# A GRU behind a mixture of experts: the order of VectorE's waits, and idle matmuls in every chunk

## The chip, the cores and the metric

The kernel runs on one core of a Trainium2 chip. The metric is the time of one execution on the device in microseconds (us); the time of the kernel before is the median of 3 runs.

## The reference

The input x has 2 sequences of 1024 tokens with 256 features. A first layer adds to each token the output of a mixture of experts (four experts and a shared branch, each 256 to 1024 to 256 with gelu). The experts' weights come from one gate per sequence, the two best of four, and two experts are masked over a third of the tokens each:

```
for e in range(E):
    h = gelu(x @ ew1[e] + eb1[e]);  y = h @ ew2[e] + eb2[e]
    out = out + w_be[:, e] * mask[e] * y
x = x + out + (gelu(x @ sw1 + sb1) @ sw2 + sb2)
```

A second layer is a recurrence over the 1024 tokens, whose state h has 256 features for each of the two sequences, and its output is added to x:

```
z = sigmoid(x_t @ W_z + h @ U_z + vz)
r = sigmoid(x_t @ W_r + h @ U_r + vr)
hh = tanh(x_t @ W + (r * h) @ U + vh)
h = (1 - z) * h + z * hh
```

Step t + 1 needs h of step t, and within a step hh needs r.

## The kernel before

**Stages.** The 1024 tokens are cut into 16 chunks of 64 (CT = 64, CH = 16). After a setup (x transposed, the gate computed, the first chunk's experts, weights of the recurrence split in two 16-bit parts) the recurrence runs from step s = 0 to 1023, with c = s // 64 the chunk and t = s % 64 the step in it. The weights of all experts stay on the chip.

**One step.** TensorE multiplies h by U_r (12 small matmuls at L781: for two output and two input halves the high part of h by two weight parts, and then the low part, h_low, by one), then by U_z (12 more), and later p = (1 + tanh_r) * h by U (12 more, into c_ps). The results are added in PSUM to the projections of x. ScalarE takes the tanh of each sum (L402). VectorE computes p_cur (L594) and its low part p_low (L597) after tanh r, the two parts of blend (L602, L604) after tanh z, and after tanh c the new state by one scan (L610, h_cur), then h_low (L613), half_h (L614) and the output row (L619).

**Side work.** Between the matmuls of z and those of c (window 0) and between those of c and the next step's r (window 1) TensorE has slots for the next chunk's work: one unit in window 0, two in window 1. The units, in a list SIDE written out ahead, are the halves of the up- and down-projections of 40 hidden tiles (UP at L688, DOWN at L706, 128x128 f32), their bias (L717) and the projections of x onto the gates (PROJECT, L722). Steps 0 to 55 hold the experts' units, steps 57 to 60 the projections. Every 16 steps (t = 1, 17, 33, 49) window 1 also holds a TURN, the transposes of 16 finished output rows (L728). No unit stands in window 1 of step 55, in both windows of step 56 and in both windows of steps 61, 62 and 63. ScalarE runs a gelu (L396) for each finished up-projection after the tanh of c, and GpSimd scales the hidden tile by the expert's weight (L275).

**The last chunk** has no next chunk. There each window ends in idle matmuls at L813 (a 128x128 bf16 identity by constants, into a bank whose content nobody needs): one of 256 columns in window 0, two of 512 in window 1. Other chunks have none.

**Order and waits.** Each engine runs its own list in order. preact counts the finished gate sums, act_done the tanhs, part_ready the parts of p and h, blended the blends and half_h. VectorE's p_cur, blend and scan each wait for two of these, written one after the other: first for VectorE's own earlier result (part_ready or blended), then for ScalarE's tanh (act_done, at L593, L601 and L609). TensorE's first weight load of c waits for p_cur, that of r for the scan.

Of the kernel before, what the change touches and what calls it, by code (L numbers as in the profile page):

```python
# [16 lines left out]
GATES = 3  # L17
R, Z, C = range(GATES)
# [6 lines left out]
STEPS = 16  # L25
# [11 lines left out]
def moe_gru_kernel(nc, x, cond, gate_w, gate_b, time_w, time_b, ew1, eb1, ew2, eb2, sw1, sb1, sw2, sb2,  # L37
                   w_z, u_z, c_z, b_z, w_r, u_r, c_r, b_r, w_h, u_h, c_h, b_h, branch_mask, out):
    B, T, D = x.shape
    E, _, H = ew1.shape  # L40
    BR = E + 1
    KC = D // P
    CT = TOKENS
    CH = T // CT
# [38 lines left out]

    UP, DOWN, BIAS, TURN, PROJECT = "up", "down", "bias", "turn", "project"
    SIDE = {(t, w): [] for t in range(CT) for w in range(2)}
    for t in range(1, CT, STEPS):
        SIDE[t, 1].append((TURN, 0, 0))
    units = []
    for i in range(BR * HT + LAG):
        if i < BR * HT:  # L90
# [32 lines left out]
    with ctx:  # L123
# [6 lines left out]
        def sem(name):  # L130
            return ctx.enter_context(nc.semaphore(name))
# [122 lines left out]
        act_done = sem("act_done")  # L254
# [172 lines left out]
        def _(dve):  # L427
# [151 lines left out]
            def side(c, t, window):  # L579
                if c == CH - 1:  # L580
                    return
                if (t, window) in SEEDS:
                    seed(c + 1, *SEEDS[t, window])
                if t == RESIDUAL_STEP:
                    residual(c + 1, window)

            sq = lambda ap: ap.rearrange("p (m b) -> p m b", b=B)
            for s in range(T):
                c, t = divmod(s, CT)
                parts = s * PARTS_STEP  # L590

                dve.wait_ge(part_ready, parts + H_HIGH)
                dve.wait_ge(act_done, s * GATES + R + 1)  # L593
                dve.scalar_tensor_tensor(p_cur[:, :, 0:B], sq(tanh_r), 1.0, sq(h_now), ALU.add, ALU.mult  # L594
                                         ).then_inc(part_ready, 1)
                dve.wait_ge(part_ready, parts + PARTS_STEP + P_HIGH)
                dve.tensor_tensor(p_low[:, :, 0:B], p_cur[:, :, 0:B], p_bits[:, :, 1:2 * B:2], ALU.subtract  # L597
                                  ).then_inc(part_ready, 1)

                dve.wait_ge(blended, (s + 1) * BLEND_STEP)  # L600
                dve.wait_ge(act_done, s * GATES + Z + 1)  # L601
                dve.scalar_tensor_tensor(blend_v[:, :, 0], tanh_z, 1.0, half_s[:, :], ALU.add, ALU.mult  # L602
                                         ).then_inc(blended, 1)
                dve.scalar_tensor_tensor(blend_v[:, :, 1], tanh_z, 1.0, half_h[:, :], ALU.subtract, ALU.mult  # L604
                                         ).then_inc(blended, 1)
                side(c, t, 1)

                dve.wait_ge(blended, (s + 1) * BLEND_STEP + 2)
                dve.wait_ge(act_done, s * GATES + C + 1)  # L609
                dve.tensor_tensor_scan(h_cur[:, 0, :], cand, blend[:, :], 0.0, ALU.mult, ALU.add  # L610
                                       ).then_inc(part_ready, 1)
                dve.wait_ge(part_ready, parts + PARTS_STEP + H_HIGH)
                dve.tensor_tensor(h_low[:, 0, :], h_now, h_high, ALU.subtract).then_inc(part_ready, 1)  # L613
                dve.tensor_scalar(half_h[:, :], h_now, -0.5, None, ALU.mult).then_inc(blended, 1)  # L614

                body, row = divmod(s, STEPS)
                if row == 0 and body >= 2:
                    dve.wait_ge(turned, body - 1)
                last = dve.scalar_tensor_tensor(  # L619
                    out_feat[:, body % 2, :, row * B:(row + 1) * B], sq(h_now), h_unscale[:, :],  # L620
                    feat[:, :, s * B:(s + 1) * B], ALU.mult, ALU.add)
                if row == STEPS - 1:
                    last.then_inc(body_added, 1)

                if t < CT - 1:
                    side(c, t + 1, 0)

        @block.tensor
        def _(pe):
# [50 lines left out]
            def up(c, i, k):  # L680
                e, j = TILES[c][i]
                n = TILE0[c] + i
                if k == 0:
                    if c <= 1 and j == 0:
                        pe.wait_ge(up_in[e], 16)
                    if n >= 2:
                        pe.wait_ge(gelu_done, n - 1)
                last = mm(up_ps[n % 2][:, 0:COLS], up_w[:, e, k, j * P:(j + 1) * P],  # L688
                          feat[:, k, c * COLS:(c + 1) * COLS], start=(k == 0), stop=(k == KC - 1),
                          skip_group_check=True)  # L690
                if k == KC - 1:
                    last.then_inc(up_done, 1)

            def down(c, i, m):
                e, j = TILES[c][i]
                n = TILE0[c] + i
                if m == 0:
                    if c <= 1 and j == 0:
                        pe.wait_ge(down_in[e], 16)
                    if e == E:  # L700
                        pe.wait_ge(gelu_done, n + 1)
                    elif c == 0:
                        pe.wait_ge(scaled_first, SCALED[n])
                    else:
                        pe.wait_ge(scaled, SCALED[n])
                last = mm(y_ps[:, m * COLS:(m + 1) * COLS], down_w[:, e, j, m * P:(m + 1) * P],  # L706
                          hidden[:, n % TILES_HELD, :], start=False, stop=(m == KC - 1), skip_group_check=True)
                if m == KC - 1:
                    last.then_inc(down_done, 1)

            def output_bias(c, m):
                if m == 0:
                    if c > 0:
                        pe.wait_ge(feat_ready, c * KC)
                    if c <= 1:
                        pe.wait_ge(rows_made, c + 1)
                mm(y_ps[:, m * COLS:(m + 1) * COLS], bias2_rows[:, m * P:(m + 1) * P],  # L717
                   branch_rows[:, c * COLS:(c + 1) * COLS], start=(m == 0), stop=False, skip_group_check=True)

            def project(c, g, m, k):  # L720
                at = (c % 2) * REGION + m * COLS
                mm(gate_ps[g][:, at:at + COLS], wx[:, g, k, m * P:(m + 1) * P], feat[:, k, c * COLS:(c + 1) * COLS],  # L722
                   start=False, stop=False, skip_group_check=True)

            def turn_body(n):
                pe.wait_ge(body_added, n + 1)
                for k in range(KC):
                    last = pe.transpose(rows_ps[:, k * P:(k + 1) * P], out_feat[:, n % 2, k, :], ident[:, :])  # L728
                last.then_inc(turned, 1)
# [54 lines left out]
            def side(c, t, window):  # L784
                for what, *of in SIDE[t, window]:
                    if what == TURN:
                        n = c * BODIES + t // STEPS
                        if n > 0:

                            pe.wait_ge(blended, (c * CT + t + 1) * BLEND_STEP + 2)  # L790
                            if n > 1:
                                pe.wait_ge(turned_copied, n - 1)
                            turn_body(n - 1)
                    elif c < CH - 1:
                        i, k = of[0], of[1]
                        if what == UP:
                            up(c + 1, i, k)
                        elif what == DOWN:
                            down(c + 1, i, k)
                        elif what == BIAS:  # L800
                            output_bias(c + 1, k)
                        else:
                            g, m, k = of
                            if m == 0 and k == 0:
                                pe.wait_ge(feat_ready, (c + 2) * KC)
                                pe.wait_ge(seeded, (c + 2) * GATES * KC)
                            if g == Z and k == 0:

                                pe.wait_ge(act_done, (c * CT + t) * GATES + Z + 1)
                            project(c + 1, g, m, k)  # L810
                if c == CH - 1:
                    for _ in range(1 + window):
                        mm(up_ps[0][:, 0:IDLE_FILL[window]], ident16[:, :], keep_warm[:, 0:IDLE_FILL[window]],  # L813
                           start=True, stop=True, skip_group_check=True)

            for s in range(T):
                c, t = divmod(s, CT)
# [52 lines left out]
```

## Time and profile before

| | us |
|---|---|
| median of 3 runs | 2193.73 (2191.86 to 2194.32) |
| the profiled execution's own time | 2188.36 |
| its span in the profile | 2186.6 |
| first scan (L610) starts at | 68.43 |
| last scan starts at | 2182.25 |
| TensorE busy with matmuls | 2097.8 (96%) |
| VectorE busy | 1225.8 (56%) |
| ScalarE busy | 690.5 (32%) |
| GpSimd busy | 216.9 (10%) |

Times inside the profile count from the start of its span. PE is TensorE's matmuls, PEld its weight loads, DVE is VectorE, ACT ScalarE, POOL GpSimd. Durations of matmuls are modelled, so the starts are the better guide there. The granted clock (PEclk) is that of TensorE, as a share of full speed (2.4 GHz); 0.50 is 1.2 GHz. A view of stretches gives for each stretch its length, then for each engine the busy time with the number of instructions in brackets, then the granted clock, the share of the DMA engines and GB/s. Since each step has one scan, the scans in a stretch count its steps. DMA plays no part after the setup: 3 to 5 GB/s.

### The profile page before, as it was taken

The page shows a single profiled execution, that of the slowest core. Times are in us where ns is not written, and L with a number is a line of the kernel's source. Part 1 is how long each engine was busy: PE and PEld are TensorE (multiplying, and loading weights), DVE is VectorE, ACT ScalarE, POOL GpSimd, SP SyncE. Part 2 cuts the span into 40 slices and gives each one's busy share as a digit, 9 for nine tenths or more (in the row PEclk, how much of TensorE's full clock was granted, in tenths as well). Part 3 has the DMA queues.
Part 4 walks back from the last instruction along what each step waited for, and adds up shares of the span by engine and source line. Part 5 has one row for each costly group of instructions (what it writes and reads, how often), then busy time and mean ns, then how long its engine had stood idle before and what let it go on. Part 6 is the DMA issues. An engine that isn't in the chain of part 4 may idle for free.

```text
span 2186.6 us, 102353 instructions
## 1 busy us (share of the span) xinstructions
PE 2097.8 (96%) x42772; PEld 1805.8 (83%) x42772; DVE 1225.8 (56%) x8413; ACT 690.5 (32%) x3780; POOL 216.9 (10%) x520
## 2 busy tenths in 40 slices
PE   8899999999999999999999999999999999999998
PEld 8788888888888888888888888888888888888655
DVE  4465655556565564655656555565555656556554
ACT  3232323323233232333323233232332323333222
POOL 2210101001010010101101011010100101011000
PEclk9998988979799797998989989798897989979899
DMA  7000000000000000000000000000000000000000
GB/s 276 3 4 4 5 3 4 5 3 5 3 5 4 3 4 4 4 4 4 4 4 5 4 4 4 4 5 3 4 5 3 4 4 4 4 4 4 4 4 4
DMA packets 16908, 23.66 MB, mean 11 GB/s; under 512 B 3584, under 2 KB 15159, under 8 KB 16444
## 3 DMA queue, kind: packets, MB, share of 16 engines
q1 hardware_dynamic: 15280, 17.05, 2.2%
q8 instruction: 334, 5.47, 1.0%
q14 instruction: 130, 1.06, 0.2%
q10 hardware_dynamic: 1164, 0.07, 0.0%
HBM read 15.01 MB, written 2.10 MB: 8 GB/s over the span
## 4 chain that ended last, share of the span: by engine, by line
PE 91%; DVE 3%; ACT 2%; issue 2%; POOL 1%; DVEq 0%; ACTq 0%
PE r_ps L781 20%; PE c_ps L781 18%; PE up_ps L688 17%; PE y_ps L706 16%; PE z_ps L781 13%; ACT rc_tanh_ps L402 2%; PE c_ps L722 1%; PE r_ps L722 1%; DVE h_cur L610 1%; PE z_ps L722 1%; DVE p_cur L594 1%; PE y_ps L717 1%; PE z_tanh_ps L728 1%; POOL uf L340 0%; ACT hidden L396 0%
## 5 line engine op out<-in xcount | busy, mean ns | idle before, releaser
L688 PE MATMUL up_ps<-feat,up_w 128*128 128x128 f32 x2528 | 550.9, 319 | 2.3 <-ACT hidden L396 1.0
L706 PE MATMUL y_ps<-hidden,down_w 128*128 128x128 f32 x2528 | 528.3, 307 | 0.0
L610 DVE TENSOR_TENSOR_SCAN h_cur<-rc_tanh_ps,blend 128x8 f32<-128x8 f32 x1024 | 177.6, 173 | 484.8 <-ACT rc_tanh_ps L402 483.5
L781 PEld LDWEIGHTS r_ps<-h_cur,u_high 128*128 128x128 f16 x4096 | 260.4, 98 | 223.5 <-DVE h_cur L610 223.3
L781 PE MATMUL r_ps<-h_cur,u_high 128*128 128x20 bf16 (+5 forms) x4096 | 355.3, 181 | 47.8 <-DVE h_cur L610 42.4
L688 PEld LDWEIGHTS up_ps<-feat,up_w 128*128 128x128 f32 x2528 | 389.5, 205 | 9.6 <-ACT hidden L396 8.9
L402 ACT ACTIVATE rc_tanh_ps<-r_ps 128x4 f32<-128x4 f32 x1024 | 161.8, 158 | 729.2 <-PE r_ps L781 729.1
L781 PE MATMUL c_ps<-p_cur,u_high 128*128 128x40 bf16 (+10 forms) x4096 | 363.6, 186 | 20.1 <-DVE p_cur L594 14.5
L706 PEld LDWEIGHTS y_ps<-hidden,down_w 128*128 128x128 f32 x2528 | 369.0, 194 | 3.3 <-issue 2.2
L594 DVE SCALAR_TENSOR_TENSOR p_cur<-rc_tanh_ps,h_cur 128x4 f32<-128x4 f32 x1024 | 166.9, 163 | 364.3 <-ACT rc_tanh_ps L402 359.5
L781 PEld LDWEIGHTS c_ps<-p_cur,u_high 128*128 128x128 f16 x4096 | 263.6, 98 | 107.6 <-DVE p_cur L594 39.0
L781 PE MATMUL c_ps<-p_cur,u_mid 128*128 128x40 bf16 (+10 forms) x4096 | 346.3, 182 | 0.0
L402 ACT ACTIVATE rc_tanh_ps<-c_ps 128x4 f32<-128x4 f32 x1024 | 161.8, 158 | 583.0 <-PE c_ps L781 583.0
L781 PE MATMUL r_ps<-h_cur,u_mid 128*128 128x20 bf16 (+5 forms) x4096 | 338.3, 178 | 0.0
L781 PE MATMUL z_ps<-h_cur,u_high 128*128 128x20 bf16 (+5 forms) x4096 | 337.5, 178 | 0.0
L781 PE MATMUL z_ps<-h_cur,u_mid 128*128 128x20 bf16 (+5 forms) x4096 | 336.9, 178 | 0.0
L275 POOL TENSOR_TENSOR hidden<-hidden,expert_w 128x128 f32<-128x128 f32 (+3 forms) x416 | 163.1, 394 | 1572.2 <-ACT hidden L396 1572.2
L781 PEld LDWEIGHTS c_ps<-p_cur,u_mid 128*128 128x128 f16 x4096 | 269.6, 99 | 5.8
L781 PEld LDWEIGHTS r_ps<-h_cur,u_mid 128*128 128x128 f16 x4096 | 263.0, 98 | 6.3 <-issue 0.3
L614 DVE TENSOR_SCALAR half_h<-h_cur 128x4 f32<-128x4 f32 x1024 | 267.4, 261 | 0.5
L781 PE MATMUL c_ps<-p_low,u_high 128*128 128x40 f16 (+10 forms) x4096 | 264.5, 181 | 0.2
L781 PEld LDWEIGHTS z_ps<-h_cur,u_high 128*128 128x128 f16 x4096 | 254.3, 97 | 0.0
(138 smaller groups left out, 3063.4 us busy)
## 6 DMA issues: line engine op xcount, KB each, us to landing
up_w<-in_L_cond_ew SPq DMA_DIRECT2D x4, 1024.0 KB, 9.3
down_w<-in_L_cond_ew SPq DMA_DIRECT2D x4, 1024.0 KB, 11.0
x_rows<-in_x SPq DMA_DIRECT2D x8, 256.0 KB, 4.4
out<-out_rows SPq DMA_DIRECT2D x128, 16.0 KB, 1.8
up_w<-in_L_cond_sw SPq DMA_DIRECT2D x1, 1024.0 KB, 12.1
down_w<-in_L_cond_sw SPq DMA_DIRECT2D x1, 1024.0 KB, 13.6
cf<-in_L_cond_C_r SPq DMA_DIRECT2D x1, 256.0 KB, 5.8
cf<-in_L_cond_C_z SPq DMA_DIRECT2D x1, 256.0 KB, 5.9
```

The source lines that it names most:

```text
L275: ins = engine.tensor_tensor(cols, cols, w, ALU.mult)
L402: act.activation((tanh_r, tanh_z, c_now)[g].rearrange("p (m b) -> p m b", b=B), gate_v[g][:, c % 2, :, t, :], ACT.Tanh, scale=0.5 / GAIN). ...
L594: dve.scalar_tensor_tensor(p_cur[:, :, 0:B], sq(tanh_r), 1.0, sq(h_now), ALU.add, ALU.mult).then_inc(part_ready, 1)
L610: dve.tensor_tensor_scan(h_cur[:, 0, :], cand, blend[:, :], 0.0, ALU.mult, ALU.add).then_inc(part_ready, 1)
L614: dve.tensor_scalar(half_h[:, :], h_now, -0.5, None, ALU.mult).then_inc(blended, 1)
L688: last = mm(up_ps[n % 2][:, 0:COLS], up_w[:, e, k, j * P:(j + 1) * P], feat[:, k, c * COLS:(c + 1) * COLS], start=(k == 0), stop=(k == KC ...
L706: last = mm(y_ps[:, m * COLS:(m + 1) * COLS], down_w[:, e, j, m * P:(m + 1) * P], hidden[:, n % TILES_HELD, :], start=False, stop=(m == KC ...
L717: mm(y_ps[:, m * COLS:(m + 1) * COLS], bias2_rows[:, m * P:(m + 1) * P], branch_rows[:, c * COLS:(c + 1) * COLS], start=(m == 0), stop=Fal ...
L722: mm(gate_ps[g][:, at:at + COLS], wx[:, g, k, m * P:(m + 1) * P], feat[:, k, c * COLS:(c + 1) * COLS], start=False, stop=False, skip_group ...
L728: last = pe.transpose(rows_ps[:, k * P:(k + 1) * P], out_feat[:, n % 2, k, :], ident[:, :])
L781: return mm(gate_ps[g][:, at:at + width], w[:, g, k, m * P:(m + 1) * P], moving, start=False, stop=last_of_sum, skip_group_check=True)
```

## The change

On VectorE the two waits ahead of p_cur, ahead of the first blend and ahead of the scan change places: the one for ScalarE's tanh (act_done) is now written first, the one for VectorE's own result second. On TensorE a slot with nothing in it but perhaps a TURN (real == 0) gets idle matmuls in every chunk, where before only the last chunk had them: one of 256 columns in window 0, two of 512 columns in window 1, and one fewer in a window that has a turn. The latter holds in the last chunk too, whose four windows with a turn so lose one of their two idle matmuls. TURNS lists the slots with a turn.

```diff
-    for t in range(1, CT, STEPS):
-        SIDE[t, 1].append((TURN, 0, 0))
+    TURNS = [(t, 1) for t in range(1, CT, STEPS)]
+    for slot in TURNS:
+        SIDE[slot].append((TURN, 0, 0))
...
+                dve.wait_ge(act_done, s * GATES + R + 1)
                 dve.wait_ge(part_ready, parts + H_HIGH)
-                dve.wait_ge(act_done, s * GATES + R + 1)
                 dve.scalar_tensor_tensor(p_cur[:, :, 0:B], sq(tanh_r), 1.0, sq(h_now), ALU.add, ALU.mult
                                          ).then_inc(part_ready, 1)
...
+                dve.wait_ge(act_done, s * GATES + Z + 1)
                 dve.wait_ge(blended, (s + 1) * BLEND_STEP)
-                dve.wait_ge(act_done, s * GATES + Z + 1)
                 dve.scalar_tensor_tensor(blend_v[:, :, 0], tanh_z, 1.0, half_s[:, :], ALU.add, ALU.mult
                                          ).then_inc(blended, 1)
...
+                dve.wait_ge(act_done, s * GATES + C + 1)
                 dve.wait_ge(blended, (s + 1) * BLEND_STEP + 2)
-                dve.wait_ge(act_done, s * GATES + C + 1)
                 dve.tensor_tensor_scan(h_cur[:, 0, :], cand, blend[:, :], 0.0, ALU.mult, ALU.add
                                        ).then_inc(part_ready, 1)
...
-                if c == CH - 1:
-                    for _ in range(1 + window):
+
+                real = 0 if c == CH - 1 else sum(what != TURN for what, *_ in SIDE[t, window])
+                turning = (t, window) in TURNS
+                if real == 0 or c == CH - 1:
+                    for _ in range(1 + window - turning):
                         mm(up_ps[0][:, 0:IDLE_FILL[window]], ident16[:, :], keep_warm[:, 0:IDLE_FILL[window]],
                            start=True, stop=True, skip_group_check=True)
```

## Rows read from the trace of the kernel before

**Rows 1.** The page: TensorE's busy tenths and granted clock in 40 slices.

```profile
PE   8899999999999999999999999999999999999998
PEclk9998988979799797998989989798897989979899
```

**Rows 2.** Stretches: opening, openings and ends of chunks, middles, last chunk.

```profile
68.43:76.90 8.47, 7.94 (x169) 6.90 (x167) 4.79 (x32) 2.99 (x16) 1.56 (x4) 1.00 0.01 2
329.18:343.52 14.34, 14.24 (x212) 12.67 (x212) 6.20 (x40) 3.82 (x21) 1.56 (x4) 0.50 0.01 3
346.03:443.37 97.34, 96.63 (x2057) 83.42 (x2055) 58.20 (x398) 33.74 (x185) 10.81 (x27) 1.00 0.02 4
443.37:462.77 19.40, 16.23 (x352) 14.46 (x353) 9.83 (x74) 4.27 (x27) 0.00 (x0) 0.75 0.01 2
1144.13:1241.35 97.22, 96.19 (x2054) 83.14 (x2052) 58.17 (x400) 33.57 (x184) 10.41 (x26) 1.00 0.02 4
1807.32:1903.94 96.62, 96.06 (x2060) 83.30 (x2056) 58.44 (x399) 33.56 (x185) 10.40 (x26) 1.00 0.02 4
2063.12:2182.25 119.13, 107.92 (x2347) 67.33 (x2346) 62.40 (x480) 29.35 (x183) 0.00 (x0) 1.00 0.02 4
```

**Rows 3.** Waits: engine, line, releaser: total us, times, longest us.

```profile
DVE h_cur L610 <- ACT rc_tanh_ps L402: 483.5, 1010, 1.0
DVE p_cur L594 <- ACT rc_tanh_ps L402: 359.5, 987, 12.2
PEld r_ps L781 <- DVE h_cur L610: 223.3, 911, 0.9
PEld up_ps L688 <- ACT hidden L396: 8.9, 16, 0.6
```

**Rows 4.** Timeline of one step at full clock: start, us, engine, instruction.

```profile
1100.77 0.16 ACT L402 ACTIVATE rc_tanh_ps<-c_ps 128x4 f32<-128x4 f32 x1 [0.52 <-PE c_ps L781]
...
1101.03 0.17 DVE L610 TENSOR_TENSOR_SCAN h_cur<-rc_tanh_ps,blend 128x8 f32<-128x8 f32 x1 [0.45 <-ACT rc_tanh_ps L402]
...
1101.76 0.16 ACT L402 ACTIVATE rc_tanh_ps<-r_ps 128x4 f32<-128x4 f32 x1 [0.55 <-PE r_ps L781]
...
1101.88 0.47 PE L688 MATMUL up_ps<-feat,up_w 128*128 128x128 f32 x2
1102.02 0.16 DVE L594 SCALAR_TENSOR_TENSOR p_cur<-rc_tanh_ps,h_cur 128x4 f32<-128x4 f32 x1 [0.41 <-ACT rc_tanh_ps L402]
...
1102.24 0.19 PE L781 MATMUL c_ps<-p_cur,u_high 128*128 128x40 bf16 x1
1102.28 0.18 PE L781 MATMUL c_ps<-p_cur,u_mid 128*128 128x40 bf16 x1
```

**Rows 5.** Line L593: instruction, count, ns min/median/max, first and last start.

```profile
L593 DVEq EVENT_SEMAPHORE  x1024: 21/21/21, 67.4 to 2181.2; - x171
```

**Rows 6.** Timeline in the setup: a feat copy and the reduction behind it.

```profile
12.00 0.63 ACT L379 ACTIVATE feat<-z_tanh_ps 128x512 f32<-128x512 f32 x1 [0.21 <-PE z_tanh_ps L641]
12.66 0.86 DVE L461 TENSOR_REDUCE seg_part<-feat 128x4 f32<-128x680 f32 x1 [0.76 <-ACT feat L379]
```

**Rows 7.** Timeline of TensorE in chunk 1, step 4: side pair, then r.

```profile
204.89 0.49 PE L706 MATMUL y_ps<-hidden,down_w 128*128 128x128 f32 x2
205.22 0.18 PE L781 MATMUL r_ps<-h_cur,u_high 128*128 128x20 bf16 x1
205.25 0.18 PE L781 MATMUL r_ps<-h_cur,u_mid 128*128 128x20 bf16 x1
```

**Rows 8.** Timeline of scans at half clock: without idle matmuls, and with them.

```profile
458.29 0.17 DVE L610 TENSOR_TENSOR_SCAN h_cur<-rc_tanh_ps,blend 128x8 f32<-128x8 f32 x1 [0.55 <-ACT rc_tanh_ps L402]
460.41 0.17 DVE L610 TENSOR_TENSOR_SCAN h_cur<-rc_tanh_ps,blend 128x8 f32<-128x8 f32 x1 [0.55 <-ACT rc_tanh_ps L402]
...
2058.46 0.17 DVE L610 TENSOR_TENSOR_SCAN h_cur<-rc_tanh_ps,blend 128x8 f32<-128x8 f32 x1 [0.55 <-ACT rc_tanh_ps L402]
...
2061.15 0.17 DVE L610 TENSOR_TENSOR_SCAN h_cur<-rc_tanh_ps,blend 128x8 f32<-128x8 f32 x1 [0.22 <-ACT rc_tanh_ps L402]
```

## The prediction

> **What bounds the kernel now.** I read the page first. TensorE is busy 96% of the span, which seems to say that only less matmul work can help, but the line of its granted clock beside it is not even: it stands at 9 to 10 tenths with a dip to 7 about every two and a half slices, and a chunk of 64 steps lasts about as long [rows 1]. So I cut the span by stage and counted the scans (L610, one for each step) in each stretch [rows 2]. With side work and the full clock (1.00 of full speed, 2.4 GHz) 49 steps take 97.34, 97.22 and 96.62 us in three chunks, 1.981 us a step. In the last nine steps of a chunk, six of which have slots without side work, the mean clock is 0.75 and nine steps take 19.40 us (2.16 each). In the next opening the clock is 0.50 (1.2 GHz) and five steps take 14.34 us (2.87 each), though TensorE has all its side work again. The last chunk has no side work anywhere and idle matmuls in its place: 60 steps in 119.13 us, 1.986 each, the clock at 1.00 throughout.
>
> The step therefore does not depend on how much TensorE has to do at full clock: 1.98 us both with side work (TensorE busy 96.63 of 97.34 us) and with the lighter idle matmuls (107.92 of 119.13 us) [rows 2]. A fixed length under different loads is a chain of latencies. The list of waits names it: VectorE waits for ScalarE's tanh 483.5 us ahead of the scan and 359.5 us ahead of p_cur, and TensorE's weight load then waits for h_cur 223.3 us [rows 3]. The timeline of one step gives its links [rows 4]: tanh of c starts at 1100.77 and ends at 1100.93, the scan starts at 1101.03; tanh of r runs from 1101.76 to 1101.92, p_cur starts at 1102.02, and c's first matmul at 1102.24. Both hand-overs from ScalarE to VectorE take 0.10 us.
>
> **The waits on VectorE.** The line of the second of each pair of waits (L593, the tanh's semaphore) is an instruction of its own on VectorE's queue, 1024 times, 21 ns each [rows 5]; so the wait written first rides on the arithmetic instruction, and the one written second is this separate instruction in front of it. In the kernel now the late event (tanh) is the separate one: VectorE must see it pass and only then start p_cur, 0.10 us after the tanh's end. The change swaps the roles at three places (L594, L602, L610). A wait for ScalarE that rides on the instruction is in the trace too: in the setup a feat copy ends at 12.00 + 0.63 = 12.63 and the reduction that waits for it starts at 12.66, 0.03 us later [rows 6]. So a hand-over should fall from 0.10 to 0.03 us, by 0.07. The bounds: nothing, if the riding wait behaves otherwise in this dense loop, and 0.08 by the rounding of these rows; I take 0.07, because the row is the same pair of engines. The part_ready and blended waits that now come as instructions of their own are for VectorE's own results, done half a microsecond before the tanh, and their 21 ns pass while VectorE is idle; if they were late, each would cost its 21 ns. Queued behind each are p_low, h_low and the rest of the step; they only come earlier. The third place (L602, blend) is not on the chain: its result is needed by the scan half a microsecond later. It counts as nothing.
>
> What is late next? After the scan, TensorE: its weight load waited 223.3 us for h_cur in 911 steps, 0.245 us each [rows 3], so 0.07 fits whole. Ahead of c there is less. The pair of side matmuls starts at 1101.88 and c's first and second matmuls come at 1102.24 and 1102.28, 0.36 and 0.40 later [rows 4]. Where TensorE is the bound, the same pair starts at 204.89 and the next matmuls at 205.22 and 205.25, 0.33 and 0.36 later [rows 7]; there the pair follows another f32 pair and lasts 0.49, here it follows a bf16 matmul and lasts 0.47, so here 0.34 would do. p_cur can come 0.04 to 0.06 us earlier before the side work is the bound, with perhaps all 0.07 where the weight load is hidden. I take 0.065. Per step 0.07 + 0.065 = 0.135 us, bounds 0 and 0.14 us.
>
> In sentences the rest can do without: the Trainium skill, "Advanced Engine Details and Errata", gives 50 to 100 ns for a sequencer that reads a semaphore's value. By it two such reads a step, 1024 times, would be an estimated 102 to 205 us against the 138 us of the rows; the rows lie inside.
>
> **The idle matmuls.** Slots without side work are the second slot of step 55, both of 56 and both of 61, 62 and 63: nine in each of 15 chunks, 4 with one 256-column matmul and 5 with two of 512 columns, so 14 matmuls and as many weight loads a chunk, 210 in all; the last chunk loses four (one in each slot with a turn). At full clock they cost nothing, since the last chunk keeps 1.986 us a step with just these in every slot [rows 2]; that cover is the same latency chain, with p_cur now 0.07 earlier, and a 256-column fill ends before f32 side work does. What they should bring is the clock: the last chunk holds 1.00 for 119 us on recurrence and fill alone, and side steps hold it for 97 us [rows 2], so no slot would be left in which TensorE does less than something that was seen to hold it. Then the opening also runs at full clock. How that looks chunk 0 shows, which opened at 1.00: its steps 1 to 4 take 8.47 us [rows 2], so steps 2 to 4 take 8.47 - 1.97 = 6.50. This is no clock: the up-projections stand close there, and TensorE waits for ScalarE's gelu once a chunk, 8.9 us in 16 waits [rows 3], and for longer bias units. Of these three steps I take off only one hand-over each: 6.50 - 0.21 = 6.29. The four dropped matmuls in the last chunk gain under 0.1 us.
>
> **The sum**, against the profiled execution (span 2186.6, its own time 2188.36 us):
> - to the first scan 68.43 - 0.14 = 68.3;
> - 1023 further steps, of which 15 x 3 = 45 are the crowded ones of the openings: 978 x (1.981 - 0.135) = 978 x 1.846 = 1805.4;
> - 15 x 6.29 = 94.4;
> - after the last scan 2186.6 - 2182.25 = 4.35, unchanged.
>
> That is a span of 1972.4, and with the 1.8 us outside it 1974.2. The runs' median of 2193.73 lies 5.4 above the profiled execution; with a steadier clock I expect a smaller distance and take 2: **1976 us**. Of the 214 us gained some 135 come from the waits and some 77 from the clock.
>
> **Rivals.**
> 1. The clock still falls at every chunk's end, so the idle matmuls do nothing. For it: it falls now although TensorE is busy 16.23 of 19.40 us there [rows 2]. Against it: the last chunk. Steps at half clock are bound by TensorE and gain little from the waits. Of 1024 steps some 850 are at full clock (all but about eleven a chunk) and gain 0.135 us each, 115 us: 2188.4 - 115 = 2073, less a little for the others: about 2071. The Trainium skill, "TensorE: Matmul & The Clock Gate" (section "Why this matters for your kernels"), puts drops of the clock down to idle gaps between bursts of matmuls. By that rule alone it would not fall here at all, since the weight load's waits in these steps are fractions of a microsecond, and fillers would have nothing to mend; the trace disagrees, so I give the rule little weight.
> 2. It holds at the chunk's end but dips in the openings: five steps at half clock in 14.34 us [rows 2] instead of the 9.9 that the sum has (6.29 and two of 1.846), 15 x 4.4 = 66 us: 2042 if in all, about 2000 if in a third of them.
> 3. The waits bring nothing, because VectorE's start after the tanh takes 0.10 us whichever wait rides on it (the change doesn't do what it says): 68.4 + 978 x 1.981 + 15 x 6.5 + 4.4 + 1.8 = 2109.5.
> 4. Slower: the clock does not hold, and each fill then runs at half clock. In the last chunk's beginning, at half clock, a step with fill takes 2061.15 - 2058.46 = 2.69 us, while one without any takes 460.41 - 458.29 = 2.12 [rows 8]. 0.57 us in five steps (56, 61 to 63 and the one after 55) of 15 chunks is 43 us: about 2232. It decides the sign only if a hand-over gains less than 43 / 2048 = 21 ns.
>
> **How the numbers follow.** The forecast (full clock, both waits) has 0.75 with an own range of 1950 to 1995; rival 2 has 0.10, rival 1 0.08, rival 3 0.05, rival 4 0.02. The range of 1948 to 2045 takes in the forecast and rival 2 and leaves about 0.15 outside; its low end is a step of 1.82 us (both hand-overs 0.07 to 0.08 and fewer stalls). About 0.2% is what a measurement of this kernel can tell from no change. All cases but the fourth are far below: faster 0.97, same 0.01, slower 0.02.
>
> **What would show it.** In the profile after: the separate wait instruction at the part_ready line instead of the tanh's, and 0.03 us from a tanh's end to p_cur and to the scan; 1.84 to 1.85 us a step in the middle of a chunk; the line of the granted clock at 9 or full without the regular 7s; about 400 idle matmuls (192 + 206); the list's wait of TensorE for h_cur nearly as large and for p_cur still small. I am wrong if the step stays near 1.98 (the waits), if c's first matmul follows the side pair with no gap and the step stands above 1.86 (TensorE as the bound), or if stretches at 0.50 remain in the chunks' ends or openings.

## The result and the profile after

| | us |
|---|---|
| kernel before, beside these runs | 2193.10 (4 runs, 2191.86 to 2194.32) |
| changed kernel | 1969.23 (4 runs, 1968.59 to 1972.54) |
| ratio | 0.8982, 95% interval 0.8967 to 0.8998 |
| profiled execution of the changed kernel, its span | 1969.39, 1967.6 |

The change takes off 10.2%; 1976 us was forecast, with a range of 1948 to 2045. Most lines of the code have moved down by one: the separate wait L593 is now L594, p_cur L595, the scan L611, the small matmuls L782, the idle matmuls L817.

The page, TensorE's busy tenths and granted clock in 40 slices. The regular 7s of [rows 1] are gone:

```profile
PE   8899999999999999999999999999999999999998
PEclk9999999999999999999999999999999999999999
```

Stretches as in [rows 2] (length, then busy time and count of PE, PEld, DVE, ACT, POOL, granted clock, DMA share, GB/s): chunk 0's steps 1 to 4; then, each of seven steps, an opening at part of the clock (chunk 2) and one at the full clock (chunk 5); then 48 steps of chunk 5's middle, the nine behind them (from the scan of step 55 to that of the next chunk's step 0, called the last nine below), and 58 steps of the last chunk.

```profile
66.37:74.48 8.11, 7.58 (x168) 6.89 (x168) 4.48 (x32) 2.99 (x16) 1.60 (x4) 1.00 0.01 2
302.68:317.39 14.71, 14.48 (x296) 13.28 (x296) 8.11 (x56) 5.22 (x28) 2.35 (x6) 0.88 0.02 5
660.23:673.85 13.62, 13.39 (x296) 12.14 (x296) 8.10 (x56) 5.22 (x28) 2.35 (x6) 1.00 0.02 5
673.85:761.90 88.05, 87.98 (x2016) 81.72 (x2016) 55.44 (x390) 33.06 (x181) 10.42 (x26) 1.00 0.02 5
761.90:778.30 16.40, 16.13 (x364) 12.88 (x366) 9.75 (x75) 4.27 (x27) 0.00 (x0) 1.00 0.01 2
1850.67:1957.08 106.41, 101.77 (x2237) 64.59 (x2265) 60.36 (x464) 28.78 (x178) 0.00 (x0) 1.00 0.02 5
```

A step of the middle is 88.05 / 48 = 1.834 us instead of 1.981, and one of the last chunk 106.41 / 58 = 1.835. The nine steps at a chunk's end take 16.40 us (1.82 each) at a clock of 1.00, where they took 19.40 at 0.75. The opening takes 13.62 us where its first five steps alone took 14.34. In 8 of the 15 chunks that have side work the clock still falls once in the opening, in step 4 and for 3.4 us, as in the second stretch, and costs 14.71 - 13.62 = 1.1 us. Such a short fall is called a dip below.

The last chunk's last three steps stand in a line of their own. The clock falls there in step 61, although that chunk has its idle matmuls in every slot:

```profile
1957.08:1963.08 6.00, 5.52 (x115) 3.82 (x117) 3.16 (x25) 1.42 (x9) 0.00 (x0) 0.63 0.01 4
```

It costs 0.6 us (steps 55 to 63 of that chunk take 17.0 us here and 16.4 in the repeated run below, where the clock holds). A fall in steps 59 to 62 of the last chunk is also in the profiles of e2, e3, e4, e5 and e10 below and in none of the others, so the idle matmuls hold the clock nearly always, not always. Their weight loads (L817) count 398, as forecast.

The line of the separate wait and the list of waits. The separate wait has moved from the tanh's line (L593 in [rows 5]) to the line of part_ready, and VectorE waits less than in [rows 3]:

```profile
L594 DVEq EVENT_SEMAPHORE  x1024: 21/21/21, 53.4 to 1961.2; - x171
```

```profile
DVE h_cur L611 <- ACT rc_tanh_ps L403: 379.9, 1008, 0.8
DVE p_cur L595 <- ACT rc_tanh_ps L403: 289.7, 975, 11.6
PEld r_ps L782 <- DVE h_cur L611: 71.9, 152, 0.6
```

TensorE's wait for h_cur, 223.3 us in 911 waits before, seems to be gone from nearly all steps. It is not: the list leaves out idle times of 0.15 us and less, and this one has fallen from 0.18 us to 0.11 in the middle of a chunk. The first weight load of r still comes 0.05 us after the scan's end, before (1101.03 + 0.17 = 1101.20) and after (995.58 + 0.17 = 995.75):

```profile
1101.26 0.10 PEld L781 LDWEIGHTS r_ps<-h_cur,u_high 128*128 128x128 f16 x1 [0.17 <-DVE h_cur L610]
...
995.80 0.10 PEld L782 LDWEIGHTS r_ps<-h_cur,u_high 128*128 128x128 f16 x1
```

The timeline of one step, the counterpart of [rows 4]. The tanh of r ends at 994.47 + 0.16 = 994.63 and p_cur starts at 994.66; the tanh of c ends at 995.54 and the scan starts at 995.58: 0.03 and 0.04 instead of 0.10 and 0.10. The side pair starts at 994.59 and c's first two matmuls at 994.89 and 994.92, 0.30 and 0.33 later instead of 0.36 and 0.40:

```profile
994.47 0.16 ACT L403 ACTIVATE rc_tanh_ps<-r_ps 128x4 f32<-128x4 f32 x1 [0.76 <-PE r_ps L782]
...
994.59 0.47 PE L707 MATMUL y_ps<-hidden,down_w 128*128 128x128 f32 x2
994.66 0.16 DVE L595 SCALAR_TENSOR_TENSOR p_cur<-rc_tanh_ps,h_cur 128x4 f32<-128x4 f32 x1 [0.34 <-ACT rc_tanh_ps L403]
...
994.89 0.18 PE L782 MATMUL c_ps<-p_cur,u_high 128*128 128x40 bf16 x1
...
994.92 0.18 PE L782 MATMUL c_ps<-p_cur,u_mid 128*128 128x40 bf16 x1
...
995.38 0.16 ACT L403 ACTIVATE rc_tanh_ps<-c_ps 128x4 f32<-128x4 f32 x1 [0.45 <-PE c_ps L782]
...
995.58 0.17 DVE L611 TENSOR_TENSOR_SCAN h_cur<-rc_tanh_ps,blend 128x8 f32<-128x8 f32 x1 [0.38 <-ACT rc_tanh_ps L403]
```

### The profile page after: what moved, and what is told of

Its sections match the earlier page's. It is cut to its first block, busy times and chain, and to the rows that moved or that the text cites. A ratio compares the mean times of both kernels' runs of the same rounds, so it can differ in the third digit from the quotient of the medians.

```text
span 1967.6 us, 102687 instructions
## 1 busy us (share of the span) xinstructions
PE 1936.1 (98%) x42900; PEld 1730.1 (88%) x42978; DVE 1188.4 (60%) x8413; ACT 689.9 (35%) x3780; POOL 216.6 (11%) x520
## 4 chain that ended last, share of the span: by engine, by line
PE 96%; issue 1%; POOL 1%; DVE 1%; ACT 1%; ACTq 0%; DVEq 0%
PE r_ps L782 20%; PE up_ps L689 18%; PE y_ps L707 18%; PE c_ps L782 16%; PE z_ps L782 16%; PE up_ps L817 4%; PE c_ps L723 1%; PE r_ps L723 1%; PE z_ps L723 1%; PE z_tanh_ps L729 1%; PE y_ps L718 1%; POOL uf L339 0%; POOL uf L341 0%; ACT hidden L397 0%; POOL wx L349 0%
## 5 line engine op out<-in xcount | busy, mean ns | idle before, releaser
L689 PE MATMUL up_ps<-feat,up_w 128*128 128x128 f32 x2528 | 519.2, 304 | 3.8 <-ACT hidden L397 3.8
L707 PE MATMUL y_ps<-hidden,down_w 128*128 128x128 f32 x2528 | 520.2, 303 | 0.0
L611 DVE TENSOR_TENSOR_SCAN h_cur<-rc_tanh_ps,blend 128x8 f32<-128x8 f32 x1024 | 177.3, 173 | 381.4 <-ACT rc_tanh_ps L403 379.9
L782 PEld LDWEIGHTS r_ps<-h_cur,u_high 128*128 128x128 f16 x4096 | 249.6, 96 | 162.6 <-DVE h_cur L611 71.9
L689 PEld LDWEIGHTS up_ps<-feat,up_w 128*128 128x128 f32 x2528 | 365.3, 193 | 8.7 <-ACT hidden L397 8.2
L782 PE MATMUL r_ps<-h_cur,u_high 128*128 128x20 bf16 (+5 forms) x4096 | 350.4, 180 | 3.1 <-DVE h_cur L611 0.7
L782 PE MATMUL c_ps<-p_cur,u_high 128*128 128x40 bf16 (+10 forms) x4096 | 343.3, 181 | 2.8
L595 DVE SCALAR_TENSOR_TENSOR p_cur<-rc_tanh_ps,h_cur 128x4 f32<-128x4 f32 x1024 | 166.0, 162 | 292.5 <-ACT rc_tanh_ps L403 289.7
L782 PE MATMUL c_ps<-p_cur,u_mid 128*128 128x40 bf16 (+10 forms) x4096 | 338.0, 180 | 0.0
L782 PE MATMUL r_ps<-h_cur,u_mid 128*128 128x20 bf16 (+5 forms) x4096 | 336.6, 178 | 0.0
L782 PE MATMUL z_ps<-h_cur,u_high 128*128 128x20 bf16 (+5 forms) x4096 | 336.0, 178 | 0.0
L782 PE MATMUL z_ps<-h_cur,u_mid 128*128 128x20 bf16 (+5 forms) x4096 | 335.4, 178 | 0.0
L620 DVE SCALAR_TENSOR_TENSOR out_feat<-h_cur,h_unscale,feat 128x4 f32<-128x4 f32 x1024 | 295.5, 289 | 0.0
L782 PEld LDWEIGHTS c_ps<-p_cur,u_high 128*128 128x128 f16 x4096 | 248.4, 96 | 40.6 <-DVE p_cur L595 26.7
L782 PE MATMUL c_ps<-p_low,u_high 128*128 128x40 f16 (+10 forms) x4096 | 259.5, 179 | 0.0
L782 PEld LDWEIGHTS r_ps<-h_cur,u_mid 128*128 128x128 f16 x4096 | 256.7, 96 | 1.1
L782 PEld LDWEIGHTS c_ps<-p_cur,u_mid 128*128 128x128 f16 x4096 | 256.5, 96 | 0.5
L782 PEld LDWEIGHTS z_ps<-h_cur,u_high 128*128 128x128 f16 x4096 | 251.8, 96 | 0.0
```

Of the source, the lines that this page charges most:

```text
L620: last = dve.scalar_tensor_tensor(out_feat[:, body % 2, :, row * B:(row + 1) * B], sq(h_now), h_unscale[:, :], feat[:, :, s * B:(s + 1) * ...
L782: return mm(gate_ps[g][:, at:at + width], w[:, g, k, m * P:(m + 1) * P], moving, start=False, stop=last_of_sum, skip_group_check=True)
```

## The experiments

**The two parts, each alone.** The kernel before with only the waits changed:

```diff
-                dve.wait_ge(part_ready, parts + H_HIGH)
                 dve.wait_ge(act_done, s * GATES + R + 1)
+                dve.wait_ge(part_ready, parts + H_HIGH)
...
(likewise ahead of the blend and of the scan; no idle matmuls added)
```

> The kernel before with only the order of the three waits changed. My theory: waits and clock are separate gains. The middle of a chunk falls from 1.981 to 1.834 us a step as in the changed kernel, the ends and openings of the chunks still run at half clock and gain little there: 2188 less 850 steps x 0.147 us, about 2060 us (2045 to 2075), mean granted clock 0.90 to 0.92. Rival: the shorter step packs TensorE densely enough to hold the clock without idle matmuls; then the clock is above 0.97 and the time below 1990 us.

And the changed kernel with the waits as before, so that only the idle matmuls remain:

```diff
-                dve.wait_ge(act_done, s * GATES + R + 1)
                 dve.wait_ge(part_ready, parts + H_HIGH)
+                dve.wait_ge(act_done, s * GATES + R + 1)
...
(likewise ahead of the blend and of the scan)
```

> The changed kernel with the order of the waits as before, so only the idle matmuls remain of the change. My theory: the clock holds except for short dips in openings (0.98), the step stays at 1.97 to 1.98 us: 2095 to 2112 us. Rival (the idle matmuls hold the clock only together with the shorter step): clock under 0.95 and 2150 us or more.

Measured beside the kernel before at 2191.62 us: 2053.34 us for the waits alone (ratio 0.9335, 0.928 to 0.939; the four runs go from 2030.51 to 2055.56) and 2115.52 us for the idle matmuls alone (0.9656, 0.9642 to 0.9671). Stretches of the waits-only kernel: the 48 middle steps of chunk 5, its last nine, and the seven of the next opening.

```profile
704.98:793.02 88.04, 87.81 (x2015) 81.67 (x2014) 55.41 (x391) 33.08 (x181) 10.45 (x26) 1.00 0.02 5
793.02:812.63 19.61, 17.02 (x352) 15.80 (x353) 9.88 (x74) 4.27 (x27) 0.00 (x0) 0.60 0.01 3
812.63:831.05 18.42, 18.32 (x297) 16.55 (x297) 8.19 (x56) 5.22 (x28) 2.35 (x6) 0.59 0.01 4
```

The middle is that of the changed kernel (88.04 us), the end and the opening are still at 0.60 and 0.59. The shorter step does not hold the clock. The idle-matmul kernel has the middle of the kernel before (first line of the next block) and a mean clock of 0.987; its time lies 3.5 us above the 2112 that I expected at most. So the waits are worth 138 us without and 146 us with the idle matmuls, and these 76 and 84 us: two gains that hardly touch.

**One hand-over at a time.** As the idle-matmul kernel, with only the waits ahead of p_cur, or only those ahead of the scan, changed:

```diff
+                dve.wait_ge(act_done, s * GATES + R + 1)
                 dve.wait_ge(part_ready, parts + H_HIGH)
-                dve.wait_ge(act_done, s * GATES + R + 1)
```

> As e2_fill_only, with the waits changed ahead of p_cur alone. My theory: 0.07 us a step off e2_fill_only, 70 to 75 us; TensorE's side work ahead of c ends just in time. Rival (side work in window 0 is the bound): 0.04 us a step or less, 40 us or less.

```diff
+                dve.wait_ge(act_done, s * GATES + C + 1)
                 dve.wait_ge(blended, (s + 1) * BLEND_STEP + 2)
-                dve.wait_ge(act_done, s * GATES + C + 1)
```

> As e2_fill_only, with the waits changed ahead of the scan alone. My theory: 0.07 us a step, 70 to 75 us off e2_fill_only, and the gains of e3 and e4 add up to the changed kernel within 5 us. Rival: one of the two gains is only had together with the other, so that they add up to 20 us less or more than the changed kernel has.

2037.18 us (0.9295, 0.9281 to 0.9308) and 2037.62 us (0.9298, 0.9284 to 0.9312): 78.3 and 77.9 us off 2115.52. The 48 middle steps of chunk 5, a stretch from each of the three kernels: idle matmuls alone,

```profile
722.13:817.42 95.29, 94.88 (x2017) 81.77 (x2015) 56.94 (x390) 33.09 (x181) 10.38 (x26) 1.00 0.02 4
```

with p_cur's waits,

```profile
696.98:788.57 91.59, 91.46 (x2017) 81.76 (x2015) 59.65 (x390) 33.09 (x181) 10.38 (x26) 1.00 0.02 4
```

with the scan's waits:

```profile
694.30:786.09 91.79, 91.54 (x2017) 81.72 (x2016) 55.50 (x391) 33.10 (x181) 10.41 (x26) 1.00 0.02 4
```

1.985, 1.908 and 1.912 us a step. Each hand-over gives 0.07 and a little more, and each kernel gains 3 us more than the 75 that I expected at most; side work in window 0 is no bound for p_cur. The two gains sum to 156.2 us where the changed kernel has 2115.52 - 1969.23 = 146.3, 10 us less, so the 5 us that I had allowed were too few. In the middles they do add up (95.29 - 91.59, 95.29 - 91.79 and 95.29 - 88.05: 3.70 + 3.50 = 7.20 against 7.24). The profiled executions differ in the dips of the clock instead: 8 with the idle matmuls alone (seven in openings and one in step 62 of chunk 13), 2 and 2 in these two kernels, 8 in the changed one. Summed as the gains are, that is 8 + 8 - 2 - 2 = 12 dips at some 0.9 to 1.1 us each. The openings bear it out: steps 0 to 7 of the 15 chunks take 250.2 us with the idle matmuls alone, 239.2 and 239.8 in these two kernels and 238.6 in the changed one, and 250.2 + 238.6 - 239.2 - 239.8 = 9.8.

**The third place.** The changed kernel with the waits ahead of the first blend in the old order:

```diff
-                dve.wait_ge(act_done, s * GATES + Z + 1)
                 dve.wait_ge(blended, (s + 1) * BLEND_STEP)
+                dve.wait_ge(act_done, s * GATES + Z + 1)
```

> The changed kernel with the waits ahead of the first blend (L602) in the old order. My theory: off the chain, no difference, 1966 to 1973 us. Rival: the late separate wait holds VectorE's queue ahead of the scan, and each step loses up to 0.07 us: 2000 to 2040 us.

1976.93 us (four runs, 1968.0 to 1978.61; ratio 0.9013, 0.899 to 0.9035), so the rival's 2000 is excluded, but the median is 8 us above the changed kernel, above my 1973. The profiled execution was the one of 1968.0 us: it has 3 dips of the clock where the changed kernel had 8, and a middle step that is 0.004 us longer. Two things make it so: stalls ahead of the scan that sum to 3.3 us instead of 0.9 (last section), and eight steps in which h_low, which TensorE needs for r, takes 0.39 to 0.41 us instead of 0.16. The line of h_low in this run, then in the changed kernel (duration in ns, min/median/max):

```profile
L614 DVE TENSOR_TENSOR h_low<-h_cur x1024: 161/164/405, 66.9 to 1961.8; 128x4 f16<-128x4 f32 x171
...
L614 DVE TENSOR_TENSOR h_low<-h_cur x1024: 161/165/165, 66.6 to 1963.3; 128x4 f16<-128x4 f32 x171
```

The other three executions ran at mean granted clocks of 0.984 to 0.986, where this one had 0.992. At 0.985 one execution of the changed kernel took 1972.54 us and one of these 1977.84. So some 5 us belong to the order at an equal clock, which fits 0.004 us in each of 1023 steps, and the rest of the 8 us to a lower clock, whose cause is open. The hand-over is not on the chain with its 0.07 us, but it does not count as quite nothing either.

**How much fill.** Idle matmuls of 64 and 128 columns in all chunks but the last:

```diff
+                        n_fill = IDLE_FILL[window] // (1 if c == CH - 1 else 4)
-                        mm(up_ps[0][:, 0:IDLE_FILL[window]], ident16[:, :], keep_warm[:, 0:IDLE_FILL[window]],
+                        mm(up_ps[0][:, 0:n_fill], ident16[:, :], keep_warm[:, 0:n_fill],
                            start=True, stop=True, skip_group_check=True)
```

> The changed kernel with idle matmuls of 64 and 128 columns in place of 256 and 512 in all chunks but the last. My theory: what counts is how much TensorE works, so the clock falls again in many chunk ends: granted clock 0.91 to 0.96, 2000 to 2060 us. Rival (closing the idle gap with any instruction is enough, as the rule on idle gaps would have it): as the changed kernel, 1969 us, clock 0.98 or more.

2031.44 us (0.9284, 0.9255 to 0.9313), mean clock 0.932. The last nine steps of chunk 5 and the seven of the next opening:

```profile
786.31:804.32 18.01, 16.23 (x364) 14.51 (x365) 9.81 (x75) 4.27 (x27) 0.00 (x0) 0.79 0.01 3
804.32:818.78 14.46, 14.26 (x297) 12.92 (x297) 8.11 (x56) 5.23 (x28) 2.36 (x6) 0.91 0.03 6
```

The number of instructions is that of the changed kernel, which has x364 in the same nine steps at a clock of 1.00; their length is a quarter, and the clock falls. It is not enough that something is issued in the gap.

**Where fill is needed.** Idle matmuls only in steps 61 to 63:

```diff
-                if real == 0 or c == CH - 1:
+                if (real == 0 and t > 60) or c == CH - 1:
```

> The changed kernel with idle matmuls only in steps 61 to 63 of the chunks before the last, none after step 55's first slot and in step 56. My theory: those two steps are enough for a fall of their own, as before in step 57; it is short, for the projections of steps 57 to 60 follow, and the fill then carries the clock into the next chunk: 2 to 3 us a chunk, 1995 to 2015 us, openings mostly at full clock. Rival: a fall at step 57 costs the opening too, 2030 us or more; or steps 55 and 56 are too short to matter, 1969 us.

1999.01 us (0.9134, 0.9117 to 0.9151), within the expectation. The one and a half empty steps 55 and 56 are enough to lose the clock around step 57, in 12 of the 15 chunks. Two ends of chunks, chunk 5's and chunk 7's:

```profile
776.71:794.22 17.51, 16.60 (x362) 13.95 (x363) 9.76 (x74) 4.27 (x27) 0.00 (x0) 0.90 0.01 3
1015.15:1035.46 20.31, 19.48 (x361) 16.41 (x362) 9.88 (x75) 4.27 (x27) 0.00 (x0) 0.60 0.01 2
```

With the same work and the same fill one end has 0.90 and the other 0.60: how long a fall lasts depends on more than the work in it.

**The crowded openings.** The bias units moved from before tile 3's down-projection to behind tile 1's up-projection:

```diff
-        if i == LAG:
+        if i == 1:
             units += [(BIAS, 0, 0), (BIAS, 0, 1)]
```

> The changed kernel with the two bias units placed after the up-projections of tile 1, so that those of tile 2 come after the gelu of tile 0 is done. My theory: TensorE's wait for the gelu makes step 2 long (2.22 us) and is also what the clock dips in step 4 or 5 follow. Without it step 2 falls by about 0.3 us and no chunk opens with a dip: 15 x 0.3 plus 8 dips x 1.06 us, about 1955 to 1961 us, clock 0.99. Rival: the dips follow the crowded bias steps instead; they remain, and the gain is at most 5 us, 1964 us or more.

And with both bias units in window 1:

```diff
-        if i < BR * HT:
+        if i == 1:
+            units += [(UP, 1, 0), (BIAS, 0, 1), (UP, 1, 1)]
+        elif i < BR * HT:
             units += [(UP, i, 0), (UP, i, 1)]
-        if i == LAG:
-            units += [(BIAS, 0, 0), (BIAS, 0, 1)]
+        if i == 0:
+            units += [(BIAS, 0, 0)]
```

> As e7, but both bias units in window 1, where TensorE has 0.08 us of slack ahead of r. If a bias unit costs less there than ahead of c, it is 2 to 4 us faster than e7 (1952 to 1958 us); if the crowding of a turn or an up-projection with a bias unit ahead of r costs as much, it is the same as e7 within 2 us.

1956.39 us (0.8929, 0.8913 to 0.8945) and 1955.06 us (0.8922, 0.8907 to 0.8938). The first is as long as expected, but not by the steps I named: its opening of chunk 5 takes 13.22 us, 0.40 less than 13.62, while step 2 stays at 2.21 us and steps 3 and 4 fall from 2.03 to 1.84 and 1.83. Both bias units now stand between the scans of steps 1 and 2. TensorE's wait for the gelu is gone (8.2 us in 17 waits after the change, 0.2 in one here), and the bias units cost as much in its place. In the second, steps 1 and 2 take 2.04 and 2.01 us: a bias unit costs 0.2 us beside other side work in either window, and the two kernels are 1.3 us apart, the same within the 2 us that I had named for that case.

```profile
655.62:668.84 13.22, 13.22 (x296) 12.00 (x296) 8.09 (x57) 5.28 (x28) 2.36 (x6) 1.00 0.02 5
```

The line is e7's opening of chunk 5. The dips are 2 and 1 in the two profiled executions.

**The bias units out of the openings.** Those of the chunk after next in window 1 of steps 61 and 62, in place of one idle matmul each (those of chunk 1 ahead of the recurrence), and an empty unit (REST) in step 1:

```diff
-        if i == LAG:
-            units += [(BIAS, 0, 0), (BIAS, 0, 1)]
+        if i == 1:
+            units += [(REST, 0, 0)]
...
+                if window == 1 and t in (61, 62) and c < CH - 2:
+                    output_bias(c + 2, t - 61)
+                    turning = True
```

> The changed kernel with the two bias units taken out of the openings (those of the chunk after next stand in window 1 of steps 61 and 62, in place of one idle matmul each, and chunk 1's ahead of the recurrence), and one empty unit in step 1 so that tile 2 does not wait for the gelu of tile 0. My theory: a bias unit costs 0.2 us of a step wherever it stands beside side work and nothing where it stands alone, and no step of an opening is then long: 15 x 0.38 us off e8, about 1949 us (1946 to 1952). Rival: long steps in the openings have another cause and stay; 1954 us or more.

1969.14 us (0.8995, 0.8981 to 0.9008), no faster than the changed kernel, where I expected 1949. Seven steps of chunk 5's opening, then the last nine steps of chunk 5, then the next opening:

```profile
660.23:673.07 12.84, 12.68 (x294) 11.64 (x294) 7.94 (x57) 5.29 (x29) 2.32 (x6) 1.00 0.02 5
761.11:778.46 17.35, 17.28 (x368) 14.35 (x367) 9.38 (x73) 4.27 (x27) 0.00 (x0) 0.89 0.01 3
778.46:792.16 13.70, 13.67 (x295) 12.44 (x295) 7.95 (x57) 5.29 (x29) 2.32 (x6) 0.89 0.02 5
```

The first line is what I wanted, 12.84 / 7 = 1.834 us a step with no crowded step. The second shows the price: steps 62 and 63 take 1.9 us and more, and the clock falls between the chunks, in 11 of 15. The last run gives the fill back where there is slack:

```diff
+                    n_fill = IDLE_FILL[window] if c == CH - 1 else 256 if turning else 512
                     for _ in range(1 + window - turning):
-                        mm(up_ps[0][:, 0:IDLE_FILL[window]], ident16[:, :], keep_warm[:, 0:IDLE_FILL[window]],
+                        mm(up_ps[0][:, 0:n_fill], ident16[:, :], keep_warm[:, 0:n_fill],
                            start=True, stop=True, skip_group_check=True)
```

> e10 with the idle matmul beside a bias unit cut from 512 to 256 columns and those of window 0 in the chunks before the last raised from 256 to 512 columns. e10 showed openings with every step at 1.83 us, but its steps 62 and 63 took 1.94 and 1.98 us and the clock fell around steps 63 and 0 in nearly every chunk. My theory: the bias unit (5 rows) counts little as work, so the fill beside it was too little for the clock and too long for the step; with more fill in window 0, where there is 0.18 us of slack, the clock holds and the steps are 1.83: 1944 to 1954 us, clock 0.99. Rival: a bias unit in place of a fill lets the clock fall whatever stands in window 0; 1960 us or more.

1955.48 us (0.8933, 0.8919 to 0.8948), just outside the upper end of what I expected and below the rival's 1960. The clock now falls only ahead of three openings of the profiled execution, in steps 63 and 0. It ties with e8; both beat the changed kernel by 0.7%, and e8 is the simpler.

**The changed kernel once more.**

> The changed kernel once more, beside these, for the number of clock dips in its openings and for the comparison with e5 and e10. My theory: the dips follow the long second step but come by chance, 1 to 10 in 15 chunks: 1966 to 1973 us. Rival: the dips are tied to the length of the chunk and come in the same 8 openings again.

1968.62 us (0.8993, 0.898 to 0.9005). Nine dips, in chunks 0, 1, 4, 5, 8, 9, 12, 13 and 14, where the first profile had them in 2, 3, 4, 7, 8, 9, 12 and 13. All begin in step 4. So they are neither tied to certain openings nor scattered: they come in two or three neighbouring chunks, again and again.

## Why the prediction was right, step by step

- **The hand-over from ScalarE to VectorE, 0.10 to 0.03 us:** right to the hundredth, and for the reason given. The separate wait now stands on the line of part_ready, and the setup's reduction in [rows 6], the same pair of engines with the wait riding on the instruction, was the right row to take it from. In sentences of their own: the Trainium skill's figure ("Advanced Engine Details and Errata", 50 to 100 ns for a sequencer that reads a semaphore's value) brackets the 70 ns measured, as it did the rows; that the 70 ns are such a reading no run shows.
- **p_cur capped by side work, 0.065:** the one term that I shaded was too careful. e3 gives the whole 0.07. c's matmuls now follow the side pair by 0.30 and 0.33 us; [rows 7] less 0.02 had 0.31 and 0.34 as the bound. TensorE has just been reached there: p_cur comes exactly as early as window 0 allows. That more on VectorE would bring nothing in the chunks with side work is an argument from these rows; no run tried it.
- **The step, 1.981 less 0.135 = 1.846:** it measured 1.834, and 978 steps of 0.012 are 12 us that the sum had too many. Some 5 us are the cap just named. Another 5 I had not thought of: stalls of VectorE between its separate wait and the operation behind it (last section). The remaining 2 us are not placed.
- **The idle matmuls:** right. They cost nothing at full clock, they hold it at the end of all 15 chunks with side work (16.40 us at 1.00), and e2 puts their worth at 76 us against the 77 of the sum. The argument behind it, that the last chunk holds the clock on such fill, is good for the stretch it was read from, but the fall in step 61 of the last chunk shows that it is no law.
- **The openings:** 8.11 us for chunk 0's steps 1 to 4, where the sum had 6.29 + 1.85 = 8.14. That the clock might dip there was rival 2, and it does in 8 of 15 chunks, but for 3.4 us, less than two steps: 1.1 us each instead of 4.4, 9 us in all.
- **Around the recurrence:** the first scan comes at 66.37 instead of 68.3. It lay between 64.9 and 68.2 in the profiles of the other kernels, of which only e10 and e11 put anything more (two bias units) ahead of it, so this says nothing of the change.

The deviations, -12 (step), +9 (dips) and -2 (first scan), make -5, and the span is 1967.6 against 1972.4. The median lies 0.2 us below the profiled execution; the 2 us that I added on top were not needed. So part of the closeness is luck: the step alone was off by 12 us, and dips that the sum did not have made up for most of it.

**The rivals.** Rival 1 (the clock falls anyway) is out. The Trainium skill ("TensorE: Matmul & The Clock Gate", section "Why this matters for your kernels") puts a fall down to idle gaps between bursts of matmuls. The traces do not bear this out as the whole cause: in the end of chunk 2 before, at 0.75 in [rows 2], TensorE was never idle for more than 0.53 us, and e6, with as many matmuls of a quarter of the length, has no idle time above 0.33 us in the end of its chunk 5 and a clock of 0.79 instead of 1.00. Rival 3 (the waits bring nothing) falls with e1, e3 and e4. Rival 4 needed the clock to fall. One sign in my last paragraph did not come as written: TensorE's wait for h_cur was to stay nearly as large in the list, which has 71.9 us instead of 223.3. The wait itself is shorter by just the hand-over's 0.07 us; most of the fall in the list is waits that have become too short for it.

**What stays open.** What the dips in the openings hang on. In kernels whose step 2 waits for the gelu their number in one profile was 8, 8, 9, 3, 2 and 2; without that wait 2, 1 and 3 (e10, whose clock falls at the ends of the chunks, left out, and the fall in the last chunk nowhere counted). So the wait may help them along, but it is not what decides, and my expectation of e7 named it too firmly. Why the clock fell in step 61 of the last chunk in some kernels and not in others. And why three executions with the old order ahead of the blend had a lower clock.

## What to carry to other kernels

When a chain of small operations passes between engines, look for which of an instruction's waits is a separate instruction ahead of it: written first, the wait that comes late rides on the operation, and here that was worth 0.07 us at each hand-over. Then count what else a stretch costs apart from its work: a short stretch with less TensorE work made not only its own steps long but about nine more, at half clock, and idle matmuls that fit in the engine's slack gave that back at no cost to the step, provided they were long enough. Both could be read from the trace before: a step as long under full as under light load, a granted clock by stage, and one place that already did it the other way.

## What was not expected of the hardware

At a few fixed steps VectorE takes 0.35 us longer between its separate wait and the operation behind it: in the profile of before 7 times ahead of p_cur and 9 times ahead of the scan, in the same steps in e2, e3 and e4 as far as they keep that order. Step 50 of chunk 4 in the kernel before, where the scan starts 0.45 us after the tanh's end at 698.55 instead of 0.10:

```profile
698.39 0.16 ACT L402 ACTIVATE rc_tanh_ps<-c_ps 128x4 f32<-128x4 f32 x1 [0.53 <-PE c_ps L781]
699.00 0.17 DVE L610 TENSOR_TENSOR_SCAN h_cur<-rc_tanh_ps,blend 128x8 f32<-128x8 f32 x1 [0.81 <-ACT rc_tanh_ps L402]
```

And in the changed kernel, where it starts 0.10 instead of 0.03 after it:

```profile
634.30 0.16 ACT L403 ACTIVATE rc_tanh_ps<-c_ps 128x4 f32<-128x4 f32 x1 [0.46 <-PE c_ps L782]
634.56 0.17 DVE L611 TENSOR_TENSOR_SCAN h_cur<-rc_tanh_ps,blend 128x8 f32<-128x8 f32 x1 [0.46 <-ACT rc_tanh_ps L403]
```

The separate waits explain the difference. In this step the separate wait starts at 698.59 before, 0.04 us after the tanh's end, and the scan follows it by 0.41. After the change it starts at 634.14, before the tanh of c has begun, and the scan follows by 0.42. In e5, whose blend comes later, it starts at 633.46, while the tanh runs until 633.70, and the scan follows at 633.87, again by 0.41. In all nine steps the scan comes 0.41 to 0.44 us after the separate wait, in all three kernels. So the stall is as long whatever the order, and the earlier the separate wait stands, the more of it lies under the tanh.

Counted from 0.05 us up, the stalls ahead of the scan shrink from 3.2 to 0.9 us in all, and those ahead of p_cur (2.5 us) vanish: 4.8 us of the 12 that the sum had too many. Why they fall in the same steps of the program in several kernels is open.
